# The row maxima of an attention head: turned by a transfer of single elements through DRAM, and row products begun 20 matmuls ahead

## The chip, the cores and the metric

The kernel runs on one core of a Trainium2 chip. Times are device microseconds (us) of one execution of the whole program. TensorE (PE), VectorE (DVE), ScalarE (ACT), GpSimd (POOL) and SyncE (SP, which here only issues transfers) each work through their own instructions in order and wait for one another at semaphores.

## The reference, cut to what matters

The program is two transformer layers over 2048 tokens of 128 channels. The change lies in the attention of the second layer: 16 heads of width 8, full softmax over all 2048 keys.

```
q, k = _rope(q, k)                                       # (B, 16, 2048, 8) here
scores = jnp.einsum('bhnd,bhmd->bhnm', q, k) / jnp.sqrt(jnp.asarray(d, x.dtype))
attn = jax.nn.softmax(scores, axis=-1)
out = jnp.einsum('bhnm,bhmd->bhnd', attn, v)
```

The softmax subtracts from each query's scores their maximum over all keys, so 2048 maxima are needed per head before its first exponential.

## The kernel before, in words

`attn1_block` handles the 16 heads one after the other. Each head's scores are computed twice. The first time (`rows`) queries lie on partitions: 64 matmuls of 128 queries by 512 keys, each pair read by one DVE reduction of 1024 columns (`reduce_rows`), which gives the maximum of 128 queries over half of the keys. The second time (`scores` in `step`) keys lie on partitions: 16 steps (t = 0 to 15) of 4 matmuls (c = 0 to 3), each of 128 keys by 512 queries. ACT takes the exponential of each (L1114) into `pb`, and `weigh` multiplies two steps later with the values, 4 matmuls on 32 columns of the array each, running together, into one bank (`A_B`). `s` counts steps over all heads, `s = 16h + t`.

The negated maximum enters the second product as two extra rows of the contracted operand, a high and a low part, in rows `QROWS` and `QROWS + 1` of the head's part of `qf`. For that the maxima, which the reductions leave with queries on partitions, must come into two rows of 2048 numbers. For head g this went: 64 row products, the last DVE reduction and a small one that joins the halves (`save_maxima`, L1085), two POOL instructions that split high and low into `nparts`, 128 partitions by 32 numbers (L1138, L1140), a PE transpose into a bank of PSUM (`turn_max`, L1018), an ACT copy to `nT` (`save_turned`, L1098), and two DMAs, one for each part, into `qf` (`max_rows`, L968). PE's first score product of the head waits for these (`max_rows_loaded`, L1037).

Two numbers set the order. `LEAD` says how many row products of the next-but-one head are started ahead: while PE does step s of head h, it does the row product number `n = 64 + LEAD + 4s + c`, so with `LEAD` = 12 the last row product of head h+1 stands in step t = 12 of head h, and in steps t = 13, 14 and 15 the row products belong to head h+2. The transpose of head h+1 stands in step t = 14 behind `weigh`. Before step 0 PE does the 64 row products of head 0 and `LEAD` of head 1, then `KICK` = 4 large matmuls that are used for nothing.

Where operands lie: head h has its `qf` and `kf` rows on partitions 0 to 63 if h is even, on 64 to 127 if it is odd (`group`). So the score products of head h and the row products of head h+1 use different halves of the array's rows, those of head h and of head h+2 the same half.

Score products go round three PSUM banks (`TURNING`), in the last head round seven; `take` writes this order down, and the transpose took a turn in it. Row products use four other banks in two pairs. SP's order is: loads of heads 0 to 2, `max_rows(0)`, load of head 3, and then for each h `max_rows(h+1)`, the load of head h+4 (behind `av_done`, the end of head h's `weigh`) and `move_sums(h)`, 8 small DMAs.

## Time and profile before

| | us |
|---|---|
| median of three runs | 1362.97 (1362.65 to 1365.63) |
| the profiled execution | 1365.2 |
| its span, first to last instruction | 1363.3 |
| second attention, first to last exponential | 556.2 to about 1233 |
| PE busy over the span | 1263.1 (93%) |
| ACT busy | 858.2 (63%) |
| DVE busy | 940.9 (69%) |

The profile shows one execution. 1.9 us of it lie outside the span. PE is busy nearly everywhere, but a busy PE may run one matmul at a time or two side by side on the two halves of the array, and this the share of busy time doesn't tell; the timeline does. The attention of the second layer takes half of the span, and its 16 heads look alike, so it is read from one or two heads.

### The profile page before, as it was taken

The numbers are of one execution on the slowest core, as the hardware profiler recorded it, in microseconds if no ns is written. First come the engines' busy times: TensorE is split into PE (matmuls) and PEld (weight loads), VectorE is DVE, ScalarE is ACT, GpSimd is POOL, SyncE is SP. The second block draws the span as 40 slices with busy tenths as digits, with TensorE's granted clock in tenths as the row PEclk, the third lists the DMA queues.
The fourth block names the chain that finished last, engine by engine and source line by source line (L and its number), as shares of the span: only waits on it lengthen the run. The fifth ranks groups of instructions, "written<-read, shape, count | busy, mean of one in ns | idle before, by whom it ended". The sixth has DMA issues, their size and how long they took to land. (4 is left out here: it accounts for less than half of the span.)

```text
span 1363.3 us, 21964 instructions
## 1 busy us (share of the span) xinstructions
PE 1263.1 (93%) x7908; PEld 714.0 (52%) x7908; DVE 940.9 (69%) x1637; ACT 858.2 (63%) x2394; POOL 186.2 (14%) x364
## 2 busy tenths in 40 slices
PE   4999999999979739999999999999999999994898
PEld 2677777777736423444444444444444444432566
DVE  4566656666558849788888888888888888804300
ACT  2666666665647300587778778778787877892442
POOL 3233333333370220000000000000000000001200
PEclk8999999999979865899999999999999999997899
DMA  2100000000000120000000000000000000000101
GB/s 77 71 10 9 7 4 9 9 4 1 1 2 1 48 106 16 16 16 5 19 20 19 13 8 19 20 19 11 10 19 19 19 4 2 3 4 20 36 0 31
DMA packets 22881, 24.81 MB, mean 18 GB/s; under 512 B 7773, under 2 KB 17885, under 8 KB 21470
## 3 DMA queue, kind: packets, MB, share of 16 engines
q1 hardware_dynamic: 22774, 23.42, 5.4%
q8 instruction: 63, 1.03, 0.3%
q14 instruction: 44, 0.36, 0.1%
HBM read 16.52 MB, written 5.24 MB: 16 GB/s over the span
## 5 line engine op out<-in xcount | busy, mean ns | idle before, releaser
L1076 DVE TENSOR_REDUCE rowmax<-psum 128x1 f32<-128x1024 f32 x512 | 602.8, 1219 | 97.6 <-PE psum L1003 97.5
L1114 ACT ACTIVATE pb<-psum 128x512 f32<-128x512 f32 x1024 | 531.7, 604 | 129.4 <-PE psum L1040 126.5
L1003 PE MATMUL psum<-kf,qf 64*128 64x512 f32 x1024 | 362.8, 453 | 18.8 <-DMA kf<-k_parts 14.0
L1040 PE MATMUL psum<-qf,kf 64*128 64x512 f32 x1024 | 373.6, 440 | 0.9 <-ACT pb L1114 0.9
L1040 PEld LDWEIGHTS psum<-qf,kf 64*128 64x128 f32 x1024 | 170.7, 184 | 272.2 <-ACT pb L1114 252.8
L1028 PE MATMUL psum<-pb,vx 128*32 128x512 f32 x2048 | 273.6, 606 | 0.0
L1003 PEld LDWEIGHTS psum<-kf,qf 64*128 64x128 f32 x1024 | 166.0, 194 | 70.7 <-DVE rowmax L1076 34.7
L500 ACT ACTIVATE pr<-psum,nmax 128x128 f32<-128x128 f32 x256 | 93.7, 366 | 114.4 <-DVE nmax L443 114.3
L538 POOL TENSOR_TENSOR pr<-pr,rtotal 128x256 f32<-128x256 f32 (+1 forms) x256 | 110.5, 452 | 235.7 <-DVE rtotal L451 235.7
L442 DVE TENSOR_REDUCE nmax<-psum 128x2 f32<-128x256 f32 x128 | 53.6, 419 | 65.0 <-PE psum L311 65.0
L1138 POOL CAST nparts<-nfull 128x16 fp32r<-128x16 f32 x16 | 3.1, 197 | 689.5 <-DVE nfull L1085 689.5
L339 PE MATMUL psum<-pt,vz 128*128 128x128 f32 x512 | 78.6, 276 | 0.0
L1028 PEld LDWEIGHTS psum<-pb,vx 128*32 128x32 f32 x2048 | 40.4, 108 | 69.7 <-issue 40.5
L502 ACT ACTIVATE pr<-psum,nmax 128x32 f32<-128x32 f32 x256 | 73.0, 285 | 0.0
L307 PE MATMUL psum<-kx,qs 64*128 64x160 f32 x512 | 69.8, 350 | 1.7 <-ACT pr L502 1.7
L325 PE MATMUL psum<-ident,pr 128*128 128x128 f32 x384 | 70.4, 292 | 0.8 <-POOL pr L538 0.8
L457 DVE COPY pt<-psum 128x384 f32<-128x384 f32 x128 | 67.7, 529 | 1.9 <-PE psum L325 1.7
L339 PEld LDWEIGHTS psum<-pt,vz 128*128 128x128 f32 x512 | 67.9, 193 | 0.0
L307 PEld LDWEIGHTS psum<-kx,qs 64*128 64x128 f32 x512 | 38.8, 186 | 52.8 <-ACT pr L502 39.2
L1319 ACT ACTIVATE hT<-psum,b 128x512 f32<-128x512 f32 x48 | 33.0, 687 | 42.9 <-PE psum L1334 42.6
L502 ACT ACTIVATION_READ_ACCUMULATOR pr<-psum,nmax 128x1 f32 x256 | 52.9, 207 | 0.0
L337 PE MATMUL psum<-pt,gv 128*128 128x128 f32 x256 | 51.5, 283 | 0.3 <-ACT oT L510 0.2
(195 smaller groups left out, 1271.9 us busy)
## 6 DMA issues: line engine op xcount, KB each, us to landing
qf<-q_parts SPq DMA_DIRECT2D x32, 128.0 KB
kf<-k_parts SPq DMA_DIRECT2D x32, 128.0 KB
q_parts<-parts SPq DMA_DIRECT2D x4, 512.0 KB, 2.7
k_parts<-parts SPq DMA_DIRECT2D x4, 512.0 KB, 2.7
cos<-cos_table SPq DMA_DIRECT2D x1, 1024.0 KB, 5.2
sin<-sin_table SPq DMA_DIRECT2D x1, 1024.0 KB, 6.9
attT<-acc SPq DMA_DIRECT2D x64, 16.0 KB
sums<-acc SPq DMA_DIRECT2D x64, 2.0 KB
```

What stands on the lines that cost most here:

```text
L307: nc.tensor.matmul(m.psum[:, bank + j, 0:WL], qs[half[j], b, s * P:(s + 1) * P], kx[half[j], b, s, :], start=True, stop=False)
L325: mm = nc.tensor.transpose(m.psum[:, T_B, j * P:(j + 1) * P], pr[:, w % 4, j * P:(j + 1) * P], m.ident[:, :])
L339: mm = nc.tensor.matmul(ob, vz[:, b, j, s, :], pt[:, w % 2, j * P:(j + 1) * P], start=False, stop=(j == 1))
L457: nc.vector.tensor_copy(pt[:, w % 2, :], m.psum[:, T_B, 0:TW]).then_inc(pt_saved, 1)
L500: nc.scalar.activation(pr[:, i % 4, j * P:(j + 1) * P], sc[:, 0:P], ACT.Exp, bias=nmax[:, i % 4, j:j + 1], accum_out=total[:, i % 4, j:j + 1])
L502: mm = nc.scalar.activation(pr[:, i % 4, 2 * P + j * G0:2 * P + (j + 1) * G0], sc[:, P:WL], ACT.Exp, bias=nmax[:, i % 4, 2 + j:3 + j], acc ...
L538: mm = nc.gpsimd.tensor_tensor(prw, prw, rb, ALU.mult)
L1003: mm = nc.tensor.matmul(m.psum[:, M_B + (u % 2) * 2 + n % 2, :], qf[g0:g0 + HALFP, b, t * P:(t + 1) * P], kf[g0:g0 + HALFP, b, c * BANK:(c ...
L1028: mm = nc.tensor.matmul(m.psum[c * VCOLS:(c + 1) * VCOLS, A_B, :], vx[:, h % VB, t, :], pb[:, (h * NT + t) % 3, c, :], start=(t == 0), sto ...
L1040: nc.tensor.matmul(m.psum[:, bank, :], kf[g0:g0 + HALFP, b, t * P:(t + 1) * P], qf[g0:g0 + HALFP, b, c * BANK:(c + 1) * BANK], start=True, ...
L1076: nc.vector.tensor_reduce(rowmax[:, g % 2, u // 2, u % 2:u % 2 + 1], m.psum[:, M_B + (u % 2) * 2:M_B + (u % 2) * 2 + 2, :].rearrange("p b ...
L1114: nc.scalar.activation(pb[:, s % 3, c, :], m.psum[:, bank_of[(s, c)], :], ACT.Exp, scale=SCALE).then_inc(exp_ready, 1)
```

## The change

The transpose on PE, its bank of PSUM, the ACT copy and `nT` go away. In their place SP issues one DMA from `nparts` (128 partitions by 32 numbers) to a new DRAM tensor `max_turned` (32 rows of 128 numbers), written crosswise: each of the 4096 numbers goes to an address 512 bytes from that of its neighbour. SP waits for it and then issues the two DMAs into `qf`, which now read `max_turned`. POOL waits with the next `nparts` for these DMAs, where it waited for the transpose. `LEAD` becomes 20, so that the last row product of head h+1 stands in step t = 10 of head h, and 20 instead of 12 row products of head 1 stand before step 0.

```
-        LEAD = 12
+        LEAD = 20
@@ SP, max_rows(h)
-                sp.wait_ge(nT_saved, h + 1)
+                sp.wait_ge(nparts_ready, h + 1)
+                sp.dma_start(m.max_turned.rearrange("r p -> p r"), nparts[:, :].bitcast(F32),
+                             allow_slow_non_contiguous=True).then_inc(max_turned, 16)
+                sp.wait_ge(max_turned, 16 * (h + 1))
                 for j in range(PARTS):
                     sp.dma_start(qf[g0 + QROWS + j:g0 + QROWS + j + 1, b, :].bitcast(F32),
-                                 nT[j * NT:(j + 1) * NT, :].bitcast(F32)).then_inc(max_rows_loaded, 16)
+                                 m.max_turned[j * NT:(j + 1) * NT, :]).then_inc(max_rows_loaded, 16)
@@ PE
-                        if t == NT - 2 and h + 1 < H1:
-                            turn_max(h + 1)
@@ ACT
-                    if c == 1 and t == NT - 2 and h + 1 < H1:
-                        save_turned(h + 1)
@@ POOL
                     if g >= 1:
-                        pool.wait_ge(nT_ready, g)
+                        pool.wait_ge(max_rows_loaded, g * 32)
@@ build
+            m.max_turned = nc.dram_tensor("max_turned", [PARTS * NT, P], F32, kind="Internal").ap()
```

How it moves instructions, at three places. First PE at the start of step t = 11 of head 0, from the last score product of step 10 on. L1040 and L1033 are the score products, L1003 and L1002 the row products, L1028 and L1021 `weigh`; `qk_loaded2` is waited for by the first row product of head 2. Before:

```order
L1040 MATMUL psum<-qf,kf 128x512 [waits exp1_ready]
L1003 MATMUL psum<-kf,qf 128x512
L1040 MATMUL psum<-qf,kf 128x512 [waits exp1_ready]
L1003 MATMUL psum<-kf,qf 128x512 [waits rows_reduced]
L1003 MATMUL psum<-kf,qf 128x512
L1040 MATMUL psum<-qf,kf 128x512 [waits exp1_ready]
L1028 MATMUL psum<-pb,vx 32x512 [waits exp1_ready]
```

And with the change:

```order
L1033 MATMUL psum<-qf,kf 128x512 [waits exp1_ready]
L1002 MATMUL psum<-kf,qf 128x512
L1033 MATMUL psum<-qf,kf 128x512 [waits exp1_ready]
L1002 MATMUL psum<-kf,qf 128x512 [waits rows_reduced,qk_loaded2]
L1002 MATMUL psum<-kf,qf 128x512
L1033 MATMUL psum<-qf,kf 128x512 [waits exp1_ready]
L1021 MATMUL psum<-pb,vx 32x512 [waits exp1_ready]
```

The instructions stand in the same places, but the row products from here on belong to head 2 (same half of the array as head 0) and not to head 1; before, that began in step 13.

Second, PE in step t = 14 of head 0. Before, the transpose stands behind `weigh` and takes a bank, so that a later score product waits for its ACT copy (`nT_saved`):

```order
L1028 MATMUL psum<-pb,vx 32x512 [waits exp1_ready]
L1028 MATMUL psum<-pb,vx 32x512 x3
L1018 MATMUL psum<-ident,nparts 32x128 [waits nparts_ready,exp1_ready]
L1040 MATMUL psum<-qf,kf 128x512 [waits exp1_ready]
L1003 MATMUL psum<-kf,qf 128x512 [waits rows_reduced]
L1040 MATMUL psum<-qf,kf 128x512 [waits exp1_ready]
L1003 MATMUL psum<-kf,qf 128x512
L1040 MATMUL psum<-qf,kf 128x512 [waits nT_saved]
```

With the change:

```order
L1021 MATMUL psum<-pb,vx 32x512 [waits exp1_ready]
L1021 MATMUL psum<-pb,vx 32x512 x3
L1033 MATMUL psum<-qf,kf 128x512 [waits exp1_ready]
L1002 MATMUL psum<-kf,qf 128x512 [waits rows_reduced]
L1033 MATMUL psum<-qf,kf 128x512 [waits exp1_ready]
L1002 MATMUL psum<-kf,qf 128x512
L1033 MATMUL psum<-qf,kf 128x512 [waits exp1_ready]
```

The transpose is gone, and every score product waits for an exponential alone.

Third, SP from the load of head 3 to the first `move_sums`. Before:

```order
L957 DMA qf<-q_parts 16x1x2048
L958 DMA kf<-k_parts 16x1x2048
L968 DMA qf<-nT 1x16x128 [waits nT_saved]
L968 DMA qf<-nT 1x16x128
L957 DMA qf<-q_parts 16x1x2048 [waits av_done]
```

With the change:

```order
L953 DMA qf<-q_parts 16x1x2048
L954 DMA kf<-k_parts 16x1x2048
L963 DMA max_turned<-nparts 128x32x1 [waits nparts_ready]
L967 DMA qf<-max_turned 1x2048 [waits max_turned]
L967 DMA qf<-max_turned 1x2048
L953 DMA qf<-q_parts 16x1x2048 [waits av_done]
```

The transfer of single elements and a second wait stand ahead of the two DMAs. The order on SP is otherwise as it was.

## Rows read from the trace of the kernel before

**Rows 1.** Page, costliest groups: xcount | busy us, mean ns | idle us before.

```profile
L1076 DVE TENSOR_REDUCE rowmax<-psum 128x1 f32<-128x1024 f32 x512 | 602.8, 1219 | 97.6 <-PE psum L1003 97.5
```

**Rows 2.** Timeline of ACT, head 0's end: start us, us, instruction, idle before.

```profile
589.62 2.07 ACT L1114 ACTIVATE pb<-psum 128x512 f32<-128x512 f32 x4 [0.54 <-PE psum L1040]
592.24 2.20 ACT L1114 ACTIVATE pb<-psum 128x512 f32<-128x512 f32 x4 [0.55 <-PE psum L1040]
595.12 0.27 ACT L1098 ACTIVATE nT<-psum 32x128 fp32r<-32x128 f32 x1 [0.67 <-PE psum L1018]
595.49 2.23 ACT L1114 ACTIVATE pb<-psum 128x512 f32<-128x512 f32 x4
598.54 2.06 ACT L1114 ACTIVATE pb<-psum 128x512 f32<-128x512 f32 x4 [0.82 <-PE psum L1040]
601.13 2.06 ACT L1114 ACTIVATE pb<-psum 128x512 f32<-128x512 f32 x4 [0.53 <-PE psum L1040]
```

**Rows 3.** Timeline of PE, one ordinary step of head 1.

```profile
606.01 0.49 PE L1040 MATMUL psum<-qf,kf 64*128 64x512 f32 x1
606.01 0.49 PE L1003 MATMUL psum<-kf,qf 64*128 64x512 f32 x1
...
607.62 1.07 PE L1028 MATMUL psum<-pb,vx 128*32 128x512 f32 x8
```

**Rows 4.** Timeline of PE, steps 14 and 15 of head 0.

```profile
594.95 0.50 PE L1040 MATMUL psum<-qf,kf 64*128 64x512 f32 x1
595.29 0.40 PE L1003 MATMUL psum<-kf,qf 64*128 64x512 f32 x1
...
597.01 1.07 PE L1028 MATMUL psum<-pb,vx 128*32 128x512 f32 x8
...
598.58 0.39 PE L1040 MATMUL psum<-qf,kf 64*128 64x512 f32 x1
```

**Rows 5.** Timeline of ACT, head 14's end and head 15.

```profile
1193.00 2.07 ACT L1114 ACTIVATE pb<-psum 128x512 f32<-128x512 f32 x4 [0.54 <-PE psum L1040]
...
1195.82 2.06 ACT L1114 ACTIVATE pb<-psum 128x512 f32<-128x512 f32 x4
1198.42 4.04 ACT L1114 ACTIVATE pb<-psum 128x512 f32<-128x512 f32 x8 [0.54 <-PE psum L1040]
```

**Rows 6.** Timeline of PE before step 0: row products and KICK.

```profile
545.89 2.34 PE L1003 MATMUL psum<-kf,qf 64*128 64x512 f32 x4
548.43 2.35 PE L1003 MATMUL psum<-kf,qf 64*128 64x512 f32 x4 [0.20 <-DVE rowmax L1076]
550.71 5.00 PE L1063 MATMUL psum<-xnT,ident 128*128 128x512 f32 x8
```

**Rows 7.** Timeline, head 1's maxima, from PE's weigh to SP's two DMAs.

```profile
590.71 1.07 PE L1028 MATMUL psum<-pb,vx 128*32 128x512 f32 x8
...
591.68 0.22 POOL L1140 TENSOR_TENSOR nparts<-nfull,nparts 128x16 fp32r<-128x16 f32 x1
...
595.41 1.19 SPq L968 DMA_DIRECT2D qf<-nT  x2
```

**Rows 8.** Tile nT: ns min/median/max, first and last start; time to landing.

```profile
L1098 ACT ACTIVATE nT<-psum x16: 266/266/267, 546.0 to 1195.5; 32x128 fp32r<-32x128 f32 x16
...
DMA to landing us min/median/max: 1.8/1.9/1.9
```

**Rows 9.** DMA view, 1274.8 to 1275.05 us: packets and their share of 16 engines.

```profile
DMA packets 280, 0.01 MB, mean 43 GB/s; under 512 B 261, under 2 KB 280, under 8 KB 280
...
q1 hardware_dynamic: 280, 0.01, 68.3%
```

**Rows 10.** DMA view, 33.5 to 34.5 us, during 64-element loads, with landing.

```profile
DMA packets 229, 0.00 MB, mean 1 GB/s; under 512 B 228, under 2 KB 229, under 8 KB 229
...
q1 hardware_dynamic: 229, 0.00, 11.0%
...
bks<-in_L_attn_bk SPq DMA_DIRECT2D x1, 0.2 KB, 2.1
```

More of the change, by code:

```diff
@@ L905, in attn1_block @@
         nmax_ready, nhigh_ready, nparts_ready = sem("nmax_ready"), sem("nhigh_ready"), sem("nparts_ready")
-        nT_ready, nT_saved, max_rows_loaded = sem("nT_ready"), sem("nT_saved"), sem("max_rows_loaded")
+        max_turned, max_rows_loaded = sem("max_turned"), sem("max_rows_loaded")
         st_ready, exp_ready, av_done = sem("st_ready"), sem("exp1_ready"), sem("av_done")
@@ L940, in take @@
             last_reader[bank] = (reader, count)
-        take(("max", 0), TURNING, nT_saved, 1)
         for s in range(STEPS):
@@ L945, in attn1_block @@
                 take((s, c), TURNING if s < STEPS - NT else TURNING + MAXIMA, exp_ready, s * NC + c + 1)
-                if s % NT == NT - 2 and c == 1 and s // NT + 1 < H1:
-                    take(("max", s // NT + 1), TURNING, nT_saved, s // NT + 2)
         @block.sync
@@ L1012, in free_bank @@
                 return bank_of[use]
-            def turn_max(g):
-                bank = free_bank(("max", g))
-                pe.wait_ge(nparts_ready, g + 1)
-                nc.tensor.transpose(m.psum[0:PARTS * NT, bank, 0:P], nparts[:, :].bitcast(F32), m.ident[:, :]).then_inc(nT_ready, 1)
             def weigh(h, t):
@@ L1058, in _ @@
             for n in range(LEAD):
-                if n == 4:
-                    turn_max(0)
                 rows(1, n)
@@ L1093, in _ @@
         def _(act):
-            def save_turned(g):
-                if g >= 1:
-                    act.wait_ge(max_rows_loaded, g * 32)
-                act.wait_ge(nT_ready, g + 1)
-                nc.scalar.activation(nT[:, :], m.psum[0:PARTS * NT, bank_of[("max", g)], 0:P], ACT.Copy).then_inc(nT_saved, 1)
             def save_sums(h):
```

2 lines of the change are left out of this document (removed).

## The prediction

> **What bounds the kernel now.** I read the page first. The work that the change touches is one stage, the attention of the second layer, and there PE is busy all the time, while DVE, which makes the maxima, does one reduction of 1.219 us after the other with pauses between [rows 1]. What ends a step is therefore looked for in the timelines of ACT and PE.
>
> The timeline of ACT gives the pace. ACT takes its exponentials in groups of four: c = 2 and 3 of one step, c = 0 and 1 of the next. Then it waits for PE, which is in `weigh`. From one group's start to the next is a step: 2.62, 3.25, 3.05 and 2.59 us at the end of head 0 [rows 2]. The reader should see two long steps at each end of a head, and that otherwise a step is 2.60.
>
> The timeline of PE says why. In an ordinary step the score product of this head and the row product of the next head start in the same hundredth of a microsecond, 606.01: they lie on different halves of the array and run side by side. The eight products from there to `weigh` at 607.62 take 1.61 us [rows 3]. In step 14 the row products already belong to head h+2, on the same half as head h, and they no longer pair: score product at 594.95, row product at 595.29, and `weigh` comes at 597.01, after 2.06 us [rows 4]. I call that a serial step. It costs 0.45 us by this place; by ACT's groups the one between 595.49 and 598.54 costs 3.05 - 2.60 = 0.45, and the one before costs 3.25 - 2.60 = 0.65 with the transpose in it [rows 2]. The steps at the edges, half of whose row products are of the one head and half of the other, took 2.62 and 2.59 and cost nothing [rows 2]. So with `LEAD` = 12, which puts the row products of steps 13 to 15 on the wrong half, two whole stretches are serial.
>
> What the transpose costs by itself is seen at the end of head 14. There are no row products there any more, the step is still 2.60 us (1198.42 - 1195.82), and the step with the transpose is 1195.82 - 1193.00 = 2.82 [rows 5]. The transpose is worth 0.22 us. That leaves 0.65 - 0.22 = 0.43 for the serial step it shared with head 0, near the 0.45 of its neighbour; I take 0.44. Rows 5 show one thing more: steps without row products are no shorter while the score products go round three banks. Row products that are done earlier are not paid back at the end.
>
> **The change part by part.** *Transpose, its bank and the ACT copy, removed:* once per head behind step 14, for heads 1 to 15, so 15 times 0.22 = 3.3 us won [rows 5]. The first of the sixteen copies [rows 8] lies before step 0, where PE waits for DVE anyway, and is worth nothing.
>
> *Eight more row products before step 0:* there PE is held by DVE, four row products per 548.43 - 545.89 = 2.54 us [rows 6], that is two reductions of 1.219 [rows 1] and a wait. Eight cost 5.1 us, in front of everything. Since row products that are missing at the end save nothing [rows 5], all of it stays.
>
> *Row products eight earlier in every head:* now the row products of steps 11 to 15 are of head h+2. The serial stretches grow from two to four. It holds for the heads that have a head h+2, 0 to 13: 14 heads x 2 x 0.44 = 12.3 us lost [rows 2, 4]. DVE doesn't matter to this: its two reductions need 2.44 us [rows 1], less than a serial step.
>
> *The transfer through DRAM:* hidden as long as it is in time. In the trace, head 1's `nparts` is ready at 591.68 + 0.22 = 591.90 and PE does head 1's first score product at 598.58 [rows 4, 7], 6.68 us later. With the change the last row product comes two steps earlier, and both these steps are serial, 3.04 us each, while the transpose's 0.22 goes: 6.68 + 6.08 - 0.22 = 12.5 us from `nparts` to the first product that needs it. Of these, the two DMAs into `qf` take 1.19/2 for the first issue [rows 7] and 1.9 for the second to land [rows 8], 2.5 together; they now read DRAM, and the 64-element loads from DRAM landed in 2.1 [rows 10], so 2.7. The crosswise transfer has 9.8 us. Its price isn't in the trace, only bounds for it. It moves 4096 single elements, 256 for each of 16 DMA engines. The nearest row is the load of a bias of 512 single elements, among the 280 packets that passed in 0.25 us: 16 x 250 / 280 = 14.3 ns a packet and engine, with the engines 68.3% busy [rows 9]. That gives 256 x 14.3 = 3.7 us, and with the 2.1 us that 64 elements take from issue to landing [rows 10], 5.8. From below, at 100% busy instead of 68.3%, it is 4.6. From above, the stretch of small 64-element loads had 229 packets in 1 us, 70 ns each [rows 10], which gives 20 us; but there the engines were 11.0% busy and waited for issues, so this is far above. I take 5.8: it is the one row in which a single transfer of many single elements was at work. It leaves 4 us to spare at each head, and the transfer costs nothing; it begins to cost at (9.8 - 2.1) / 256 = 30 ns an element.
>
> All rows with single elements read DRAM and write on the chip; none writes single elements to DRAM. The Trainium skill, "DMA: Bandwidth & Descriptors", section Specifications, says that below 512 B a DMA engine reads, modifies and writes; no run here shows that. An estimate by that page, with each element passing twice, would be 2.1 + 2 x 3.7 = 9.5 us, just in time. By the row the sum is the same; by the page too, but with 0.3 us to spare instead of 4.
>
> *Before step 0* the transfer has more room: the transpose of head 0, which needs `nparts`, stood ahead of the products that start at 545.89, and the first score product follows on KICK's end, 550.71 + 5.00 and now 5.1 more [rows 6]: 15 us against 5.8 + 2.7. *SP:* the wait for the transfer holds up what is queued behind it, the load of head 3 at the start and, in each head, the wait for `av_done` and then the load of head h+4 and `move_sums`. Those are released in step 1 of the next head, some 12 us after `nparts`, and the loaded rows are first used more than a head later: nothing. *POOL* waits with `nparts` for the previous head's DMAs, over a head old: nothing. If the cover of SP's wait failed, it would be because PE itself was waiting, which is the rival.
>
> **The sum.** 5.1 + 12.3 - 3.3 = +14.1 us. On the profiled execution (1365.2 with its span of 1363.3 and 1.9 around it) that is 1379.3; this execution was 2.2 above the median of the three, so on the median of 1362.97 it is 1377.1, 1.0% slower. I forecast 1377. Within this case the serial step could be 0.40 to 0.46, and the lead's products 4.9 to 5.3: 1375 to 1379, with the spread of the runs 1374 to 1381.
>
> **The rivals.**
>
> *The crosswise transfer is late.* Each microsecond over 9.8 stands in front of 15 heads, +15 us. For it: elements of 4 bytes written to DRAM are shown nowhere, they go to addresses 512 bytes apart, and half the margin is gone at 30 ns an element, twice the nearest row. Against it: at 14.3 ns the engines were not full [rows 9]. With the transfer at 12 us the kernel takes 1377 + 15 x 2.2 = 1410, with the 20 us of the upper bound 1377 + 15 x 10.2 = 1530.
>
> *The long steps belong to the transpose.* This is the one that ends faster. If not only 0.22 but all of 0.65 + 0.45 = 1.10 us of the two long steps came from the transpose's turn in the ring of three banks, which shifts every later product by one bank, then removing it wins 14 x 1.10 + 0.22 = 15.6, and against the 5.1 before step 0 the kernel takes 1352.5. In general, with x for what a serial step costs, the transpose costs 1.10 - 2x and the sum is 5.1 + 28x - 14 (1.10 - 2x) - 0.22 = 56x - 10.5: it decides from x under 0.19, and I read x = 0.44. Against it: the second long step, 595.49 to 598.54, comes after the transpose, and PE's timeline shows products one behind the other, 0.34 us apart, in it [rows 2, 4].
>
> *Serial steps cost, but half.* If half of the 0.44 were the transpose's aftermath, x = 0.22, the sum is 56 x 0.22 - 10.5 = +1.8: 1365, no change that can be told. The same rows speak against it.
>
> **How the numbers follow.** About 0.2% is what a measurement of this kernel can tell. The transfer hidden and the serial steps as read: 0.68, at 1374 to 1381. The transfer late: 0.22, most of it up to 1410. Long steps from the transpose: 0.05, at 1350 to 1356. Half: 0.05, at 1361 to 1370. The range goes from 1371 to 1408: it leaves out the two smaller cases and the far part of the late one, some 2 in 10. Faster 0.05, same 0.04, slower 0.91.
>
> **What would show it.** In the profile after: PE's timeline with unpaired score and row products from step 11 to 15 of each head up to 13, ACT's groups 3.04 apart four times and 2.60 elsewhere, none with 3.25; step 0 about 5.1 us later behind the start of the stage; the time from issue to landing of the transfer to `max_turned` near 6 us; the stage from copy to copy 42.88 us per head before ((1195.5 - 595.1)/14, [rows 2, 8]) and 42.88 + 0.88 - 0.22 = 43.5 after. It is wrong if PE waits for a DMA at the first score product of a head (late transfer), if a head is shorter than 42.9 (transpose), or if the four steps are not longer than 2.60.

## The result, and the profile after

The changed kernel takes 1539.97 us (1535.87 to 1543.19, 4 runs) against 1362.95 (1362.65 to 1365.63, 4 runs) of the kernel before: a ratio of 1.129, with an interval of 1.126 to 1.132. It is 177 us slower, where the prediction said 14. The profiled execution took 1540.76 us with a span of 1539.0; that of before had a span of 1363.3.

The page of the changed kernel, its second and fifth part. DVE's reductions are L1065 (before: L1076, [rows 1]), the score products L1033, the row products L1002, ACT's exponentials L1096.

```profile
PEclk9999999999898569899999899999899999855799
...
L1065 DVE TENSOR_REDUCE rowmax<-psum 128x1 f32<-128x1024 f32 x512 | 605.5, 1219 | 224.4 <-PE psum L1002 224.1
...
L1033 PE MATMUL psum<-qf,kf 64*128 64x512 f32 x1024 | 410.5, 467 | 103.9 <-DMA qf<-max_turned 102.4
```

A reduction takes 1219 ns as before, but DVE idles 224 us before them where it was 98 before [rows 1]. The score products have a releaser that the page of before doesn't have: PE waited 102.4 us for a DMA into `qf`. The clock row has a notch in heads 0 to 14 (8 among nines) and a trough of 5 towards the end, in the last head.

The waits over the attention of the second layer say who waits for the transfer: engine and line, releaser, us in total, times, longest.

```profile
PEld psum L1033 <- DMA qf<-max_turned: 109.7, 16, 9.3
PE psum L1033 <- DMA qf<-max_turned: 102.4, 16, 8.9
```

All sixteen heads wait. The operations of the tile `max_turned` give the price of a transfer: L963 is the crosswise one, L967 the two DMAs into `qf`.

```profile
L967 SPq DMA_DIRECT2D qf<-max_turned x32: 220/244/255, 564.2 to 1341.1; - x32
L963 SPq DMA_DIRECT2D max_turned<-nparts x16: 372/386/392, 547.1 to 1324.3; - x16
...
DMA to landing us min/median/max: 16.0/16.6/17.3
```

The crosswise transfer takes 16.6 us from issue to landing, where the prediction took 5.8. For head 1 one can follow it: the row products' maxima end in `nparts` at 598.35, and SP and PE go on as follows.

```profile
598.38 0.39 SPq L963 DMA_DIRECT2D max_turned<-nparts  x1
615.71 0.52 SPq L967 DMA_DIRECT2D qf<-max_turned  x2
```

```profile
611.08 0.39 PE L1002 MATMUL psum<-kf,qf 64*128 64x512 f32 x1
618.32 0.79 PE L1033 MATMUL psum<-qf,kf 64*128 64x512 f32 x1 [6.84 <-DMA qf<-max_turned]
```

PE had nothing left to do at 611.48 (618.32 - 6.84), 13.1 us after `nparts`; the prediction had said 12.5. The maxima came 20.0 us after `nparts`: 17.3 for the crosswise transfer and 2.6 for the two DMAs, said to be 2.7. Everything around the transfer was read rightly; the transfer itself wasn't.

ACT's timeline shows the same place, the end of head 0 and the start of head 1 (before: [rows 2]).

```profile
598.68 2.22 ACT L1096 ACTIVATE pb<-psum 128x512 f32<-128x512 f32 x4 [0.54 <-PE psum L1033]
601.72 2.21 ACT L1096 ACTIVATE pb<-psum 128x512 f32<-128x512 f32 x4 [0.82 <-PE psum L1033]
604.75 2.21 ACT L1096 ACTIVATE pb<-psum 128x512 f32<-128x512 f32 x4 [0.82 <-PE psum L1033]
607.78 2.21 ACT L1096 ACTIVATE pb<-psum 128x512 f32<-128x512 f32 x4 [0.82 <-PE psum L1033]
610.81 1.09 ACT L1096 ACTIVATE pb<-psum 128x512 f32<-128x512 f32 x2 [0.82 <-PE psum L1033]
619.20 1.09 ACT L1096 ACTIVATE pb<-psum 128x512 f32<-128x512 f32 x2 [7.30 <-PE psum L1033]
622.16 2.07 ACT L1096 ACTIVATE pb<-psum 128x512 f32<-128x512 f32 x4 [1.87 <-PE psum L1033]
```

From 598.68 to 610.81 there are four steps of 3.04, 3.03, 3.03 and 3.03, the serial steps of the forecast, and none with 3.25. Then a gap of 7.30, and behind it a second loss that no step of the prediction has: 1.87 us of idle instead of 0.54. PE's granted clock explains it. Busy times, clock and DMA share in the stretches before, in and behind the gap:

```profile
core 0: us, PE busy (x) PEld busy (x) DVE busy (x) ACT busy (x) POOL busy (x), PEclk, DMA share, GB/s
600.00:611.00 11.00, 11.00 (x61) 5.45 (x60) 8.80 (x8) 7.59 (x15) 0.00 (x0) 1.00 0.22 1
...
618.50:622.00 3.50, 3.50 (x16) 1.09 (x18) 1.23 (x1) 1.09 (x2) 0.00 (x0) 0.50 0.00 0
622.00:660.00 38.00, 37.98 (x225) 17.17 (x222) 32.89 (x29) 29.75 (x57) 0.66 (x3) 0.98 0.18 18
```

After 6.84 us of nothing PE works at a granted 0.50, that is 1.2 GHz, and then has its 2.4 GHz again: the mean is 0.50 from 618.3 to 623.4 and 1.00 from 623.5 to 660, so the full clock came back some 5 us after PE had resumed. In the last head it doesn't come back that soon. PE's timeline at the boundary from head 14 to head 15, and the windows behind it:

```profile
1334.53 0.73 PE L1033 MATMUL psum<-qf,kf 64*128 64x512 f32 x2
1344.15 1.22 PE L1033 MATMUL psum<-qf,kf 64*128 64x512 f32 x2 [8.89 <-DMA qf<-max_turned]
1345.30 1.93 PE L1021 MATMUL psum<-pb,vx 128*32 128x512 f32 x8
...
1349.16 1.93 PE L1021 MATMUL psum<-pb,vx 128*32 128x512 f32 x8
```

```profile
1350.00:1400.00 50.00, 50.00 (x160) 17.61 (x156) 0.00 (x0) 27.18 (x54) 0.00 (x0) 0.50 0.01 2
```

and the same stage of the kernel before:

```profile
1200.00:1230.00 30.00, 30.00 (x170) 11.86 (x171) 0.00 (x0) 29.52 (x59) 0.00 (x0) 1.00 0.02 3
```

PE is busy for all of the 50 us, without a pause, and its clock stays at 0.50. `weigh` takes 1.93 instead of 1.07 us [rows 3], and from one `weigh` to the next it is 3.86 us (1349.16 - 1345.30), where a step of the last head took 2.11 before.

**The account of the span**, 1539.0 - 1363.3 = 175.7 us, by the first exponential of head 0 (556.17 before, 567.36 after), the first of head 15 (1199.4, 1345.04) and the copy of the last sums (1234.38, 1409.37):

| | forecast | measured |
|---|---|---|
| stages ahead: the stage begins at 504.7 instead of 502.7 | 0 | 2.0 |
| eight more row products before step 0 | +5.1 | +5.0 |
| KICK, 5.83 instead of 5.00 us | 0 | +0.8 |
| wait for head 0's transfer | 0 | +3.3 |
| heads 0 to 14: serial steps less transposes | +9.0 | +8.5 |
| heads 1 to 14: clock after the wait, 14 x 1.33 | 0 | +19 |
| heads 0 to 14: waiting for the transfer, and what isn't told apart from it | 0 | +107 |
| last head | 0 | +29.3 |
| the rest | 0 | +0.7 |

The heads 0 to 14 took 134.5 us more together ((1345.04 - 567.36) - (1199.4 - 556.17)). Their serial steps give 14 x (4 x 0.43 - 1.10) - 0.22 = 8.5, the idle of 1.87 instead of 0.54 behind each wait gives 19 (an estimate: it was 1.59 to 1.87 from head to head), and 107 are left. PE's own waits are 102.4 - 3.3 = 99.1 of them. The other 8 aren't told apart; the first products behind each wait run at the low clock too. The 3.3 us are PE's row at step 0 [rows 6 has before]:

```profile
557.68 5.83 PE L1052 MATMUL psum<-xnT,ident 128*128 128x512 f32 x8
566.82 0.50 PE L1033 MATMUL psum<-qf,kf 64*128 64x512 f32 x1 [3.31 <-DMA qf<-max_turned]
```

KICK took longer because the full clock came later in it: the granted clock was 0.50 from 557.7 to 562.0 and 1.00 behind, where before it was 0.50 from 550.7 to 553.3 and 1.00 behind.

### The profile page after: what moved, and what is told of

It is laid out like the page before. It is cut to its first block and busy times, and to the rows that moved or that the text cites. A ratio compares the mean times of both kernels' runs of the same rounds, so it can differ in the third digit from the quotient of the medians.

```text
span 1539.0 us, 21902 instructions
## 1 busy us (share of the span) xinstructions
PE 1336.4 (87%) x7892; PEld 744.0 (48%) x7892; DVE 943.9 (61%) x1637; ACT 860.3 (56%) x2378; POOL 186.5 (12%) x364
## 5 line engine op out<-in xcount | busy, mean ns | idle before, releaser
L1065 DVE TENSOR_REDUCE rowmax<-psum 128x1 f32<-128x1024 f32 x512 | 605.5, 1219 | 224.4 <-PE psum L1002 224.1
L1096 ACT ACTIVATE pb<-psum 128x512 f32<-128x512 f32 x1024 | 536.9, 601 | 365.0 <-PE psum L1033 362.9
L1033 PE MATMUL psum<-qf,kf 64*128 64x512 f32 x1024 | 410.5, 467 | 103.9 <-DMA qf<-max_turned 102.4
L1002 PE MATMUL psum<-kf,qf 64*128 64x512 f32 x1024 | 381.7, 465 | 18.0 <-DMA kf<-k_parts 13.9
L1033 PEld LDWEIGHTS psum<-qf,kf 64*128 64x128 f32 x1024 | 189.4, 201 | 418.3 <-ACT pb L1096 263.3
L1021 PE MATMUL psum<-pb,vx 128*32 128x512 f32 x2048 | 300.9, 663 | 0.0
L1002 PEld LDWEIGHTS psum<-kf,qf 64*128 64x128 f32 x1024 | 179.4, 205 | 68.4 <-DVE rowmax L1065 32.3
L1021 PEld LDWEIGHTS psum<-pb,vx 128*32 128x32 f32 x2048 | 41.9, 112 | 83.1 <-ACT pb L1096 43.1
L1158 DVE RECIPROCAL rsums<-sums 128x512 f32<-128x512 f32 x1 | 3.4, 3355 | 92.9 <-PEq L883 92.9
L1299 ACT ACTIVATE hT<-psum,b 128x512 f32<-128x512 f32 x48 | 33.0, 687 | 43.1 <-PE psum L1314 42.9
```

What stands on the lines that cost most here:

```text
L1002: mm = nc.tensor.matmul(m.psum[:, M_B + (u % 2) * 2 + n % 2, :], qf[g0:g0 + HALFP, b, t * P:(t + 1) * P], kf[g0:g0 + HALFP, b, c * BANK:(c ...
L1021: mm = nc.tensor.matmul(m.psum[c * VCOLS:(c + 1) * VCOLS, A_B, :], vx[:, h % VB, t, :], pb[:, (h * NT + t) % 3, c, :], start=(t == 0), sto ...
L1033: nc.tensor.matmul(m.psum[:, bank, :], kf[g0:g0 + HALFP, b, t * P:(t + 1) * P], qf[g0:g0 + HALFP, b, c * BANK:(c + 1) * BANK], start=True, ...
L1065: nc.vector.tensor_reduce(rowmax[:, g % 2, u // 2, u % 2:u % 2 + 1], m.psum[:, M_B + (u % 2) * 2:M_B + (u % 2) * 2 + 2, :].rearrange("p b ...
L1096: nc.scalar.activation(pb[:, s % 3, c, :], m.psum[:, bank_of[(s, c)], :], ACT.Exp, scale=SCALE).then_inc(exp_ready, 1)
```

## The experiments

Two parts of the change were told apart first, then the transfer was taken to pieces, then the clock, and at the end what a better version would be. The kernel before ran beside each set, at medians of 1363.8 to 1364.6 us. A time without a range is of a single run. The line numbers of a variant can be off by one or by a few.

### The lead alone

```
-        LEAD = 12
+        LEAD = 20
```

on the kernel before, with transpose and copy as they were.

> The kernel before with LEAD = 20 alone; transpose and copy stay. Theory (row products on the scores' half of the array are serial): 5.1 us before step 0 and 14 x 2 x 0.44 = 12.3 in the heads, 1363.0 + 17.4 = 1380; four steps of about 3.04 us at the end of each head. Rival (the long steps came from the transpose): only the 5.1 us before step 0, 1368, and still two long steps.

Measured: 1382.69 us (1379.7 to 1384.29), ratio 1.014 (1.012 to 1.016). ACT's timeline at the end of head 0:

```profile
595.29 2.21 ACT L1114 ACTIVATE pb<-psum 128x512 f32<-128x512 f32 x4 [0.82 <-PE psum L1040]
...
598.54 2.20 ACT L1114 ACTIVATE pb<-psum 128x512 f32<-128x512 f32 x4
601.57 2.07 ACT L1114 ACTIVATE pb<-psum 128x512 f32<-128x512 f32 x4 [0.82 <-PE psum L1040]
```

The step with the transpose is 3.25 and the next 3.03, as before; two more steps of 3.03 to 3.04 stand ahead of them, without any transpose near. The long steps belong to the row products on the same half of the array, and both rivals are out: the one that gave them to the transpose and the one that gave it half of them.

### The transfer alone

```
-        LEAD = 20
+        LEAD = 12
```

on the changed kernel.

> The changed kernel with LEAD = 12 again. Theory (the transfer takes 16.6 us from issue to landing and PE waits for what it can't cover): the two serial steps less give back 12.3 us, but the cover shrinks by the same two steps of 3.04, so 15 x 6.1 = 91 us more of waiting; before step 0 nothing changes, since PE waits there either way. 1540 - 12 + 91 = 1619, and the last head again at 3.87 us a step. Rival (the time goes by something in the longer lead, not by the wait): under 1530.

Measured: 1640.58 us; a landing of 17.5, 18.1 and 18.6 (least, median, most). The transfer with the old lead is 277 us slower than the kernel before, and 100 slower than with the new lead. So the lead of 20 helps the transfer: it buys 6 us of cover per head and costs, by the experiment ahead, 18.9 in all. The 21 us above the expected 1619 are near the 15 x 1.5 us by which the landing is later here than the 16.6 that was reckoned with.

### One transfer only, at both leads

In both kernels only head 0 sends its maxima through DRAM crosswise; the other heads' two DMAs read what lies there. The second also has `LEAD` = 12.

```
                 sp.wait_ge(nparts_ready, h + 1)
-                sp.dma_start(m.max_turned.rearrange("r p -> p r"), nparts[:, :].bitcast(F32),
-                             allow_slow_non_contiguous=True).then_inc(max_turned, 16)
-                sp.wait_ge(max_turned, 16 * (h + 1))
+                if h == 0:
+                    sp.dma_start(m.max_turned.rearrange("r p -> p r"), nparts[:, :].bitcast(F32),
+                                 allow_slow_non_contiguous=True).then_inc(max_turned, 16)
+                    sp.wait_ge(max_turned, 16)
```

> The changed kernel, but the transfer to DRAM is made for head 0 alone and left out for heads 1 to 15, whose two transfers into qf then read head 0's maxima. Its time is that of the change with a transfer that costs nothing after head 0. Theory (all that is wrong in the sum is the transfer): 1363 + 14 as forecast, and 3 to 4 more for head 0, whose transfer PE awaits before step 0: 1380. Rival (the rest of the sum is wrong too): over 1390 or under 1370.

> The same with LEAD = 12: the transfer to DRAM for head 0 alone, left out for heads 1 to 15. It shows what taking the transpose and the copy away is worth by itself. Theory: -3.3 us for the transposes, and for head 0 the transfer lands at about 562, two transfers more make 564.7 where step 0 began at 555.6 before, so +9: 1363 - 3.3 + 9 = 1369, with 42.7 us a head against 42.9. Rival (long steps came from the transpose): -15.6 + 9, 1356.

Measured: 1384.59 us (1383.26 to 1386.15), ratio 1.015 (1.014 to 1.017) with the lead of 20, and 1373.34 (1369.77 to 1375.35), ratio 1.007 (1.006 to 1.008) with 12. The first stands 155 us under the changed kernel: that is what fifteen late transfers cost, and nothing else in the change costs more than 20 together. Its 20 us over before are the forecast's 14.1, 4.7 that PE waits for head 0's transfer, and about 1 in the last head. A head with a head h+2 takes 43.54 us there, forecast 43.5. The second has heads of 42.68 us against 42.91, so a head without transpose and copy gains 0.23, forecast 0.22; it loses 11 us at the start, where the late transfer has less beside it.

That 1 us of the last head comes from the banks. In the last head the score products go round seven banks, and the place in the ring goes on counting. Before, 960 score products and 16 transposes had taken a turn, 976 = 7 x 139 + 3, so the head began with the four banks that the row products had left. Without transposes it is 960 = 7 x 137 + 1: two banks come first that wait for exponentials. The prediction called the transpose's bank removed and didn't look whom it shifts.

### The crosswise side moved to the read

`max_turned` is written as it lies in `nparts`, 128 rows of 128 bytes, and the two DMAs gather single elements.

```
-                sp.dma_start(m.max_turned.rearrange("r p -> p r"), nparts[:, :].bitcast(F32),
-                             allow_slow_non_contiguous=True).then_inc(max_turned, 16)
+                sp.dma_start(m.max_turned, nparts[:, :].bitcast(F32)).then_inc(max_turned, 16)
@@
-                                 m.max_turned[j * NT:(j + 1) * NT, :]).then_inc(max_rows_loaded, 16)
+                                 m.max_turned[:, j * NT:(j + 1) * NT].rearrange("p t -> t p"),
+                                 allow_slow_non_contiguous=True).then_inc(max_rows_loaded, 16)
```

> The changed kernel with the crossing moved to the other side: nparts is written to DRAM as it lies (128 rows of 128 bytes), and the two transfers into qf read single elements, 2048 each. Theory (what is slow is writing single elements to DRAM): the write lands in 2.1 to 2.7 us, the two reads by my estimate of 14.3 ns an element in about 2.1 + 3.7 together, 8.5 in all, inside the 12.5 us that are there, so 1377. Rival (any 4096 single elements take 16 us): 18 to 19 us in all, as after, 1540.

Measured: 1640.39 us (1639.71 to 1651.87), ratio 1.205 (1.200 to 1.210): neither. The tile's landing times (least, median, most of the write and the two reads together):

```profile
DMA to landing us min/median/max: 1.4/21.8/25.7
```

The write lands in 1.4 us, the two reads in some 20 to 26. The heads wait 204.0 us for them, twice as long as for the crosswise write. Both theories had taken it that a DMA of single elements is either slow or fast; that the reads here are slow and the bias loads of [rows 9, 10] weren't says that it matters where the elements go. That called for probes.

### Probes, first set

Eight transfers follow one another at the end of the kernel before, each waited for before the next: 4096 elements of `xn` (32 per partition) unless said otherwise. They come on top of the kernel's time, which tells nothing here (1466.35 us; 1435.67 and 1405.73 for the two later sets).

```
+            probes = [(cross[0:4096].rearrange("(r p) -> p r", p=P), src),
+                      (near[0:8192].rearrange("(p r two) -> p r two", p=P, two=2)[:, :, 0], src),
...
+            for i, (dst, s) in enumerate(probes):
+                sp.dma_start(dst, s, allow_slow_non_contiguous=True).then_inc(stored, 16)
+                sp.wait_ge(stored, 16 * (i + 1))
```

> The kernel before with eight transfers of single elements ahead of the store of the output, each waited for, so their time is added (about 80 us) and read one by one: (1) 4096 elements to DRAM crosswise, 512 bytes apart; (2) 4096 to DRAM, 8 bytes apart; (3) crosswise with rows 576 bytes apart; (4) 2048 crosswise; (5) 1024 crosswise; (6) 4096 on the chip, 8 bytes apart; (7) 4096 read crosswise from DRAM; (8) 2048 pairs of elements crosswise to DRAM. Theory (writes to DRAM of less than some size have a fixed cost each): (1) to (3) 16.6, (4) 9.4, (5) 5.7, (6) and (7) about 6, (8) 9.4 us. Rival A (the distance of 512 bytes makes them collide): (2) or (3) about 6. Rival B (each single element costs 57 ns wherever it goes): (6) and (7) 16.6.

Measured, as the time from one issue to the next on SP:

| | us |
|---|---|
| 1: 4096 crosswise into DRAM, as in the change | 17.98 |
| 2: 4096 into DRAM, those of a partition 8 bytes apart | 21.03 |
| 3: as 1, with rows 576 bytes apart instead of 512 | 22.35 |
| 4: 2048 crosswise | 11.34 |
| 5: 1024 crosswise | 11.49 |
| 6: 4096 from one tile on the chip to another, 8 bytes apart | 4.16 |
| 7: 4096 from DRAM, crosswise, into 128 partitions | 4.20 |
| 8: 2048 pairs (8 bytes) crosswise into DRAM | 9.27 |

The rows of 1 and of 7, each with the issue that follows:

```profile
1357.24 0.38 SPq L1385 DMA_DIRECT2D probe<-xn  x1
1375.22 0.64 SPq L1385 DMA_DIRECT2D probe<-xn  x1
...
1445.59 0.37 SPq L1385 DMA_DIRECT2D xnT<-probe  x1
1449.79 0.36 SPq L1385 DMA_DIRECT2D probe<-xn  x1
```

The price is not one of single elements as such: read from DRAM or moved on the chip, 4096 take 4.2 us, even less than the 5.8 that the row of the bias load gave. Written to DRAM they take four times that. The stride of 512 bytes isn't it (3), nor do elements close together help (2). And the time hardly falls with the number: 1024 take 11.49 us, where a fixed price for each element would have made it 5.7.

### Half the elements per head

Only the high parts are sent crosswise, 2048 elements, and both DMAs into `qf` read them.

```
-                sp.dma_start(m.max_turned.rearrange("r p -> p r"), nparts[:, :].bitcast(F32),
+                sp.dma_start(m.max_turned[0:NT, :].rearrange("r p -> p r"), nparts[:, 0:NT].bitcast(F32),
```

> The changed kernel with the high parts alone carried crosswise to DRAM, 2048 elements instead of 4096; the row of low parts gets the high ones too. Theory A (a fixed time for each element written to DRAM, (16.6 - 2.1) / 4096): the transfer lands in 9.4 us, within the 9.8 there are, 1377 to 1380. Theory B (as the quiet probe of 2048 elements, 11.3 us): PE waits 0.6 to 1.5 us a head, 1386 to 1403; in both PE's clock stays up and the last head takes 2.11 us a step.

Measured: 1413.35 us, above every expectation. The landing is 10.1, 11.1, 11.7, as probe 4 had said, and PE's weight load waits only 10.1 us for it over all heads together, the last boundary included. What was missed is at the last boundary: PE's row, and the windows behind it.

```profile
1218.42 0.73 PE L1033 MATMUL psum<-qf,kf 64*128 64x512 f32 x2 [2.23 <-DMA qf<-max_turned]
```

```profile
1215.00:1220.00 5.00, 2.77 (x20) 0.75 (x12) 0.00 (x0) 2.52 (x5) 0.00 (x0) 0.95 0.01 3
1220.00:1222.50 2.50, 2.50 (x8) 1.16 (x4) 0.00 (x0) 1.19 (x4) 0.00 (x0) 0.50 0.00 0
...
1230.00:1280.00 50.00, 50.00 (x159) 17.15 (x162) 0.00 (x0) 26.57 (x53) 0.00 (x0) 0.50 0.00 1
```

2.2 us of idle were enough: from 1220 on PE has 0.50, and keeps it for the whole last head, whose steps take 3.87 us instead of 2.11. That costs 26 us. At the other boundaries PE waited 0.6 us at most, and the clock stayed up. The last boundary is the latest, since head 14 has no head h+2 and so no serial steps: its cover is about 4 x 0.43 = 1.7 us shorter than that of the other heads.

### The last head kept warm

Ten large matmuls used for nothing stand in the changed kernel ahead of head 15's first score product. They run while PE waits.

```
                 if t == 0:
+                    if h == H1 - 1:
+                        pe.wait_ge(rows_reduced, H1 * HALVES)
+                        for _ in range(WARM):
+                            nc.tensor.matmul(m.psum[:, M_B, :], m.ident[:, :], m.xnT[:, 0:BANK], start=True, stop=True)
                     pe.wait_ge(max_rows_loaded, (h + 1) * 32)
```

> The changed kernel with ten large matmuls, used for nothing, ahead of the last head's first score product, so that PE works for about 8.6 of the 9 us that it waits there for the transfer. Theory (the last head's 3.87 us a step come from PE's clock, which fell in the wait and never rose again): the last head at 2.11 us a step, 1540 - 26.5 = 1513. Rival (the pace comes from the ring of banks or from DMAs): 3.87 still, 1540.

Measured: 1510.56 us, 29.4 under the changed kernel's median. ACT still waits 8.80 us at that boundary, but the window behind it shows another clock:

```profile
1350.00:1370.00 20.00, 20.00 (x116) 7.78 (x118) 0.00 (x0) 19.65 (x39) 0.00 (x0) 1.00 0.02 4
```

So what the last head lost is its clock and not more waiting, and a little work in the gap keeps it.

### Probes, second set

The same frame, eight other shapes into DRAM.

> The kernel before with eight more transfers to DRAM ahead of the store, each waited for: (1) 4096 elements crosswise, 512 bytes apart, once more; (2) 1024 crosswise; (3) 512 crosswise; (4) one column of 128 elements, side by side; (5) 4096 elements 64 bytes apart, each partition's in its own 2 KB; (6) 4096 elements 512 bytes apart, each partition's in its own 16 KB; (7) 4096 pieces of 16 bytes crosswise; (8) 4096 pieces of 64 bytes crosswise. Theory A (elements written into the same few bytes of DRAM as others wait for one another, so that pieces of 64 bytes or elements 64 bytes apart are free of it): (5), (6) and (8) near 6 us, (1) 18, (7) between. Theory B (every small write to DRAM has a price): (5), (6) and (8) 16 us and more, like (1).

| | us |
|---|---|
| 1: 4096 crosswise | 15.94 |
| 2: 1024 crosswise | 10.54 |
| 3: 512 crosswise | 8.21 |
| 4: 128, one per partition, side by side | 7.31 |
| 5: 4096, each 64 bytes from the next | 8.66 |
| 6: 4096, each 512 bytes from the next | 7.68 |
| 7: 4096 pieces of 16 bytes crosswise | 10.05 |
| 8: 4096 pieces of 64 bytes crosswise | 4.47 |

Row 4 against rows 5 and 6 is the finding. 128 single elements side by side take nearly as long as 4096 that lie apart. And pieces of 64 bytes, sixteen times the data in the same number of pieces and in the same crosswise order, take little more than a quarter of the time. So it costs that several small writes fall on the same few bytes of DRAM. The number costs too: 4096 elements apart take 8.66 and 7.68 us where theory A had 6. From there to crosswise it is another 7 to 8 us.

### More cover

```
-        LEAD = 20
+        LEAD = 36
```

on the changed kernel: the maxima are ready four steps earlier still.

> The changed kernel with LEAD = 36, at which even the slow transfer should be covered. Theory: two more us before step 0 per four row products, so 15.2 more than with 12; eight serial stretches instead of two, 14 x 6 x 0.44 = 37; the transposes gone, -3.3; no wait for the transfer, which has 22 us and more at each head, and the last head at 2.11 us a step: 1364 + 49 = 1413. Rival (the transfer slows down with what runs beside it, or the serial steps cost more when there are more of them): over 1425.

Measured: 1411.08 us. The landing is 15.3, 16.0 and 17.0, and nobody waits for it. A head takes 45.26 us, since eight of its steps are serial. The prediction's picture of cover against landing holds; but hiding the transfer costs more than the transpose ever did.

### Probes, third set

How near is too near, whose writes collide, and does the reading side have its own limit? The first four have 128 elements, one per partition.

> The kernel before with eight more transfers ahead of the store, each waited for. 128 single elements to DRAM, one from each partition: (1) side by side, (2) 32 bytes apart, (3) 64 bytes apart, (4) 128 bytes apart. (5) 2048 elements, each partition's 16 side by side in 64 bytes of its own; (6) 1024, each partition's 8 in 64 bytes of its own, 8 bytes apart. (7) 2048 elements read crosswise from DRAM into one partition; (8) the same number read into 128 partitions, 16 side by side in each. Theory A (writes to one stretch of 64 bytes wait for one another, whichever engine they come from): (1) 7.3, (2) near 3, (3) and (4) 2.2, (5) about 7 or more, (6) less than (5). Theory B (only different engines in the same 64 bytes disturb one another): (1) 7.3, (2) 3, (5) and (6) 3. For (7) and (8): if one partition as target is what made the reads slow, 12 and 3; else both 3.

| | us |
|---|---|
| 1: side by side, 4 bytes apart | 7.41 |
| 2: 32 bytes apart | 1.41 |
| 3: 64 bytes apart | 1.40 |
| 4: 128 bytes apart | 1.40 |
| 5: 2048; the 16 of a partition side by side, in 64 bytes of their own | 11.04 |
| 6: 1024; the 8 of a partition 8 bytes apart, in 64 bytes of their own | 5.41 |
| 7: 2048 read crosswise from DRAM into one partition | 12.94 |
| 8: the same 2048 read into 128 partitions, 64 bytes in each | 1.54 |

SP's issues of 1, 2 and 3, and of 7 and 8:

```profile
1355.88 0.34 SPq L1394 DMA_DIRECT2D probe<-xn  x1
1363.29 0.33 SPq L1394 DMA_DIRECT2D probe<-xn  x1
1364.70 0.32 SPq L1394 DMA_DIRECT2D probe<-xn  x1
...
1383.95 0.62 SPq L1394 DMA_DIRECT2D xnT<-q_parts  x1
1396.90 0.33 SPq L1394 DMA_DIRECT2D xnT<-q_parts  x1
1398.43 0.39 SPq L1396 DMA_DIRECT2D out<-x  x1
```

At 32 bytes apart nothing collides. At 4 bytes eight elements share 32 bytes and it takes 6.0 us more; if they go one after the other, that is (7.41 - 1.41) / 7 = 0.86 us for each further one, an estimate. Where between 4 and 32 bytes it begins wasn't tried with 128 elements. The trace says where the 6 us lie. In 1 as in 2 there are 144 packets, the last of them through 1.0 us after the issue. Then 2 lands 0.4 us later, and 1 after 6.4 us in which no packet passes.

The rival, that only writes from different partitions disturb one another, falls with 5: there each partition has its 64 bytes for itself, and 2048 take 11.04 us, more than 4096 that lie apart (8.66).

Row 7 explains the kernel with the crosswise read: single elements into one partition are slow too, 12.94 us for 2048, where 4096 into 128 partitions took 4.20 (row 7 of the first set). Row 8 isn't its counterpart, though meant as one: its elements went in pieces of 64 bytes, 144 packets in the trace against 2064.

### The turn without single elements

DVE turns each block of 32 by 32 of `nparts` where it stands, in one instruction, and both DMAs move rows: 128 bytes each into `max_turned`, and pieces of 128 bytes out of it. `LEAD` is 12 as before.

```
+                nc.vector.transpose(turned[:, :], nparts[:, :].bitcast(F32)).then_inc(dve_turned, 1)
@@
-                sp.dma_start(m.max_turned.rearrange("r p -> p r"), nparts[:, :].bitcast(F32),
-                             allow_slow_non_contiguous=True).then_inc(max_turned, 16)
+                sp.dma_start(m.max_turned, turned[:, :]).then_inc(max_turned, 16)
@@
+                    sp.dma_start(qf[g0 + QROWS + j:g0 + QROWS + j + 1, b, :].bitcast(F32).rearrange("o (t q p) -> o t q p", q=4, p=32),
+                                 m.max_turned.rearrange("(q j t) p -> j t q p", q=4, j=PARTS)[j]).then_inc(max_rows_loaded, 16)
```

> A version meant to beat both: LEAD = 12; the maxima are turned on DVE in blocks of 32 by 32 behind the next reduction, written to DRAM as 128 rows of 128 bytes (1.4 us in the run that did so), and read into qf as 64 pieces of 128 bytes a row. Theory: 0.2 + 1.4 + 2.6 us lie within the 6.4 that are there, nothing waits, and the transposes' 15 x 0.22 are won: 1364.5 - 3.3 = 1361, last head at 2.11 us a step. Rival (the two transfers take over 5 us): each head waits, and the clock falls in the last head, 1390 and more.

Measured: 1361.51 us (1360.78 to 1363.5), ratio 0.998 (0.997 to 0.999). The timeline over all engines for head 1, from DVE to the DMAs into `qf`, and the tile's landing times:

```profile
591.86 0.20 DVE L1081 STREAM_TRANSPOSE turned<-nparts 128x32 f32<-128x32 f32 x1
...
592.09 0.33 SPq L964 DMA_DIRECT2D max_turned<-turned  x1
...
593.51 1.24 SPq L967 DMA_DIRECT2D qf<-max_turned  x2
```

```profile
DMA to landing us min/median/max: 1.4/2.0/2.1
```

The same way through DRAM, with the same bytes, lands in 1.4 us instead of 16.6 when each write is 128 bytes in one piece. PE's transpose is gone from every head, and nobody waits for a DMA. It is worth 2.6 us, 15 x 0.22 less the 1 us of the shifted ring.

### The lead made shorter

```
-        LEAD = 12
+        LEAD = 8
```

on the kernel before.

> The kernel before with LEAD = 8 alone. Theory (serial steps): 2.5 us less before step 0 and one serial stretch less in 14 heads, -6.2; the transpose now waits 0.3 us for nparts, +4: 1364.5 - 4.5 = 1360. The copy and the transfers into qf come 0.3 us later, where 0.7 us were to spare. Rival (that margin isn't there): PE waits at each head and the last head runs at the low clock, 1395.

Measured: 1362.13 us (1359.18 to 1363.47), ratio 0.998 (0.997 to 0.999), 2 us less, where 4.5 were expected. The first exponential comes 1.6 us earlier (554.55 instead of 556.17) and not 2.5, since KICK took 6.46 us instead of 5.00. A head takes 42.8 us, hardly less than 42.9, since the transpose is now so near behind the maxima that PE waits 0.28 us for POOL. In the direction in which the change went, the kernel before was already past its best.

### The three together

`LEAD` 10, the turn on DVE, and the ring of the last head begun at the free banks:

```
-                take((s, c), TURNING if s < STEPS - NT else TURNING + MAXIMA, exp_ready, s * NC + c + 1)
+                take((s, c), TURNING if s < STEPS - NT else TURNING[2:] + MAXIMA + TURNING[:2], exp_ready, s * NC + c + 1)
```

> The version with the turn on DVE, with LEAD = 10 and the ring of seven banks in the last head turned so that it begins with the four fresh ones, as it did before. Theory: 1.3 us less before step 0, 1.1 us less around the last head's first steps (2.94 + 2.77 + 2.38 us there become 2.60 + 1.98 + 2.38), and 0.3 us still to spare for the two transfers: 1361.5 - 2.4 = 1359. Rival (the transfers come late by some tenths): a wait at each head, 1365, or with the clock falling in the last head 1390.

Measured: 1359.12 us (1357.65 to 1360.46), ratio 0.9965 (0.9951 to 0.9978): faster than both kernels, 5.5 us faster than the one before beside it. ACT's row at the start of the last head:

```profile
1191.68 4.25 ACT L1106 ACTIVATE pb<-psum 128x512 f32<-128x512 f32 x8 [0.54 <-PE psum L1033]
```

Eight exponentials run in one row, as in [rows 5], where the version with the turn on DVE and the old ring idles 0.22 and 0.71 us. From the first exponential of head 14 to the copy behind head 15 the two take 77.0 and 78.0 us. The ring's 1 us is thereby shown in the trace; the three parts weren't timed apart in this setting.

## Why the prediction was wrong

The sum of the prediction was right in its parts and wrong in the one term that it set to zero.

**Held.** The serial steps: four of 3.03 to 3.04 per head, forecast 3.04, and a head of 43.54 us where no transfer is late, forecast 43.5. The transpose: 0.23 us per head by the kernel with one transfer, forecast 0.22. The row products before step 0: 5.0, forecast 5.1. The last leg, the two DMAs into `qf`: 2.6, forecast 2.7. The cover of the transfer: 13.1 us from `nparts` to the end of PE's work at head 1, forecast 12.5. With the lead alone on the old kernel +18.9 us were measured; the forecast's two terms for it are 5.1 + 12.3 = 17.4, and KICK took 0.7 more, 5.70 instead of 5.00.

**The step that failed** is the price of the crosswise transfer: "That gives 256 x 14.3 = 3.7 us, and with the 2.1 us that 64 elements take from issue to landing [rows 10], 5.8". It was 16.6. The row was one of single elements read from DRAM into many partitions, and for that the price is near (probe 7: 4.20 us for 4096). It was carried over to writes into DRAM, which no row showed, on the ground that it was "the one row in which a single transfer of many single elements was at work". Two things stood between. Single elements written to DRAM that lie apart, with no two in the same 64 bytes, take 7.68 to 8.66 us, (8.66 - 1.40) / 256 = 28 ns per element and engine: just inside the break-even of 30. And in the change they don't lie apart. The prediction looked at one partition's elements, which are 512 bytes from one another, and saw no neighbour; but those of eight partitions next to each other fall into the same 32 bytes. The 128 elements side by side alone show 7.3 to 7.4 us for that.

The page of before had a landing of the same bias load, and the prediction didn't use it:

```profile
b<-in_L_ffn_b1e SPq DMA_DIRECT2D x2, 2.0 KB, 3.1
```

By it (3.1 - 2.1) / 32 = 31 ns an element and engine, an estimate with the wait behind other loads in it. That is the break-even of 30, and no 4 us to spare.

The Trainium skill, "DMA: Bandwidth & Descriptors", section Specifications, has a DMA engine read, modify and write below 512 B; the prediction's estimate by it, 9.5 us, was nearer than its own 5.8, and still short. No run here shows whether the engine reads first. What the runs show is that 4096 single elements written to DRAM took 7.68 to 21.03 us and read from it into 128 partitions 4.20, and that below 512 B there is no one price: 128 rows of 128 bytes landed in 1.4 us, 4096 pieces of 64 bytes took 4.47, of 16 bytes 10.05, single elements 512 bytes apart 7.68 and crosswise 15.94 to 17.98.

The upper bound of 20 us was in the text, and set aside as "far above" because the DMA engines were 11.0% busy there. The measured 16.6 lies near that bound by luck: the row's 70 ns came from engines that waited for issues. Here they didn't. The transfer's packets in the trace, from 598 to 606 and from 606 to 615:

```profile
DMA packets 4108, 0.02 MB, mean 2 GB/s; under 512 B 4108, under 2 KB 4108, under 8 KB 4108
```

```profile
DMA packets 4, 0.00 MB, mean 0 GB/s; under 512 B 4, under 2 KB 4, under 8 KB 4
```

All but four packets are through by 606, the last by 606.3, and the transfer lands at 615.7. A price made from packets and busy shares can't contain these 9 us. This is the second thing wrong with the 14.3 ns: it counts when packets pass, and the landing isn't the last packet.

**The rival of the late transfer** had the mechanism, the place and PE's wait, at a chance of 0.22. Its price, 15 us for each microsecond over 9.8, gives 1377 + 15 x 6.8 = 1479 for 16.6, against 1540. The missing 61 us are terms that it lacks: 29 in the last head (28 by PE's clock, 1 by the ring) and 19 behind the waits of heads 1 to 14, again by the clock; 4 at step 0, with KICK; 5 that the waits and what isn't told apart from them come to more than 15 x 6.8, 1.7 of them at the last boundary with its shorter cover; the rest is the 2 us of the stages ahead and the spread of the runs. So the range was too narrow on this side twice, by the transfer's time and by what a late microsecond costs.

**The rivals on the other side** are out: the long steps are not the transpose's, neither all nor half.

**POOL and SP**: nothing, as said. SP waits up to 16.9 us for each transfer, but then still up to 9.5 us for `av_done`, and nobody waits for its later loads.

Not settled: what the DMA does in the 9 us between the last packet and the landing (the third set of probes shows such a gap, 6.4 us, when elements share 32 bytes, and 0.4 when they don't), and how the two costs (elements as such, and several in the same 32 bytes) add up: 8.7 and 6.0 give 14.7, measured were 15.3 to 18.6, and the crosswise 2048 took 11.34 and the 1024 11.49 in the same probe. It wasn't tried either what brings PE's clock back in a last head that has lost it; only that it isn't lost with work in the gap.

## What to carry to other kernels

Take the price of a DMA only from a row with the same direction, target and shape, and from issue to landing; if there is none, keep the whole range between the bounds and ask for the case at the far one. For a crosswise write look at what lies next to each element in memory, over all partitions, and not only at the stride within one; turned on an engine in blocks of 32 and written in pieces of 128 bytes, the same maxima landed in a tenth of the time. And price a wait of PE with what the clock costs behind it, above all where no second stream of matmuls follows.

## What the runs showed of the hardware that was not expected

- Single elements written to DRAM wait for one another when they fall in the same 32 bytes: 128 of them side by side took 7.41 us, 32 bytes apart 1.41. They do so too when they come from one partition (2048 in 11.04 us where each partition has 64 bytes to itself, 4096 apart in 8.66).
- Single elements into one SBUF partition are slow: 2048 took 12.94 us, and 4096 into 128 partitions 4.20.
- A transfer can land 9 us after its last packet in the trace (606.3 and 615.7). With 128 elements it was 6.4 us where they share 32 bytes and 0.4 where they don't.
- 2.2 us of idle took PE from 2.4 to 1.2 GHz (granted 0.95 in the 5 us around it, 0.50 behind). Waits of up to 0.6 us in the same run didn't. With score and row products following, the full clock was back about 5 us after PE had resumed (618.3 to 623.4); in the last head, busy without a pause at 0.50 from 1346 to 1403, it didn't come back in those 57 us.
- DVE turned 128 x 32 numbers in blocks of 32 in 0.20 us.
